# Sorting, placing and the first projections of a two-layer graph kernel in one block

## The reference, cut to what matters

```python
h = jnp.maximum(_layernorm(x, axis=-1), 0.0)
x = x + _L0_gnn_ref(h, src, dst, ...)        # two attention layers and two layer norms
h = jnp.maximum(_layernorm(x, axis=-1), 0.0)
x = x + _L1_gnn_ref(h, edge_index, edge_type_34, ...)   # means by relation, then GCN
# first attention layer, gatv2(h, ...):
fs = (x @ Ws + bs).reshape(-1, H, D)         # the two projections, 768 x 768 each
fd = (x @ Wd + bd).reshape(-1, H, D)
e = jax.nn.leaky_relu(fs[src] + fd[dst], 0.2)
logits = jnp.einsum('ehd,hd->eh', e, attn)
```

## Time and profile before

| | us |
|---|---|
| median of three executions | 3424.81 |
| the profiled execution | 3424.99 |
| its span | 3423.3 |
| TensorE busy | 2869.4 (84%) |
| VectorE busy | 2306.1 (67%) |
| ScalarE busy | 1693.3 (49%) |
| POOL busy | 1607.2 (47%) |

### The profile page before, as it was taken

The page is one execution under the profiler, slowest core; times in us unless marked ns, Lnnn a source line. Parts: engine busy times, 40 slices in busy tenths (PEclk is TensorE's granted clock), DMA queues, the critical chain, the costliest instruction groups (busy, mean ns, idle before and its releaser), DMA issues. The chain is left out here.

```text
span 3423.3 us, 59889 instructions
## 1 busy us (share of the span) xinstructions
PE 2869.4 (84%) x13554; PEld 2146.9 (63%) x13555; DVE 2306.1 (67%) x4378; ACT 1693.3 (49%) x5352; POOL 1607.2 (47%) x2067
## 2 busy tenths in 40 slices
PE   0396798889879799999676999999999995777799
PEld 0253455445445455555245999999999983555598
DVE  5234799999967688888475555555555547888743
ACT  0010799999932122333243656666566566777400
POOL 2473666566536555555112445544444445555201
PEclk6698899999989899999788999999999997989899
DMA  1332544444431355556226677777777746666411
GB/s 36 108 93 78 180 131 125 123 137 124 126 125 47 107 166 170 170 174 186 85 79 213 231 238 241 244 239 242 239 239 234 231 156 212 204 200 204 137 33 64
DMA packets 174949, 545.50 MB, mean 159 GB/s; under 512 B 55331, under 2 KB 56343, under 8 KB 174723
## 3 DMA queue, kind: packets, MB, share of 16 engines
q0 software_dynamic: 82000, 370.33, 34.5%
q1 hardware_dynamic: 72596, 128.39, 12.1%
q10 hardware_dynamic: 20304, 46.21, 4.3%
HBM read 461.31 MB, written 83.81 MB: 159 GB/s over the span
## 5 line engine op out<-in xcount | busy, mean ns | idle before, releaser
L2160 PE MATMUL pO<-wh,gT 128*128 128x384 f32 x3264 | 865.7, 339 | 22.9 <-ACT gT L2111 19.6
L770 POOL DMA_INDIRECT row<-fs_d,rec x400 | 463.3, 1158 | 392.1 <-PE pA L1295 167.8
L2160 PEld LDWEIGHTS pO<-wh,gT 128*128 128x128 f32 x3264 | 593.5, 188 | 32.1 <-ACT gT L2111 27.6
L2160 PE MATMUL pO<-wl,gT 128*128 128x384 f32 x1632 | 546.7, 335 | 0.0
L2174 DVE TENSOR_SCALAR cntge<-pT 128x768 int32<-128x768 int32 x137 | 131.2, 958 | 426.7 <-PE pT L485 234.0
L1003 ACT ACTIVATE sj<-sj 128x96 f32<-128x96 f32 x1176 | 313.2, 268 | 87.1 <-DVE sj L1120 85.9
L2111 ACT ACTIVATE gT<-cntge 128x256 fp32r<-128x256 f32 x822 | 295.3, 411 | 30.2 <-DVE cntge L2177 4.0
L2160 PEld LDWEIGHTS pO<-wl,gT 128*128 128x128 f32 x1632 | 307.7, 189 | 0.0
L770 POOL DMA_INDIRECT row<-y_d,rec x200 | 202.9, 1015 | 176.1 <-PE pR L2306 119.2
L2306 PE MATMUL pR<-row,share 128*128 128x384 f32 x384 | 169.5, 594 | 118.1 <-DVE acc L2354 65.8
L1042 PE MATMUL pS<-row,ident 128*128 128x384 f32 x400 | 179.2, 531 | 104.5 <-DVE sj L1120 64.3
(11 more groups left out here) (380 smaller groups left out, 5981.9 us busy)
## 6 DMA issues: line engine op xcount, KB each, us to landing
fdt<-in_L_gnn_W_rel_dram SPq DMA_DIRECT2D x170, 384.0 KB
startrow<-seen_d ACTq DMA_DIRECT2D x141, 320.0 KB
raw<-in_L_gnn_W_rel_dram SPq DMA_DIRECT2D x34, 384.0 KB
row<-fs_d,rec POOLq DMA_INDIRECT x400
kept_d<-fdt SPq DMA_DIRECT2D x10, 384.0 KB
kept<-kept_d SPq DMA_DIRECT2D x10, 384.0 KB
fs_d<-of SPq DMA_DIRECT2D x9, 388.0 KB
fd_d<-of SPq DMA_DIRECT2D x9, 388.0 KB
```

The source lines that it names most:

```text
L770: pool.indirect_dma_start(b["row"][u][:, j, :].bitcast(words), None, table, bass.IndirectOffsetOnAxis(ap=b["rec"][u][:, 2 * j + field:2 * ...
L2160: last = pe.matmul(pO[:, q, 0:HALF], gT[:, c, half, :].bitcast(F32R), w[:, c, lo:up].bitcast(F32R), start=c == 0 and k == 0, stop=c == KC ...
```

## The change

Stages 1, 2 and 3 become one stage with one block. The barriers between them and the clearing of semaphores there go. The helper functions (`halves` to `Signal`) move up unchanged. The buffers acc, den, cntge, rcnt and fdt are made after the merged stage instead of between the second and the third.

- SP: x(0,0) is loaded ahead of the edges, x(0,1) behind them; later loads and stores of the projections stand between the steps of the sorting.
- ScalarE issues the loads of the weights, biases and attention vector, ahead of its first norm. The weights have a semaphore each (w_in), the rest one together (v_in).
- POOL: the constants of placing and the empty row are made with the others; 20 marks ahead of the scatter by rank, 20 behind the all-reduce of the maxima, then the records and the three copies, then the last 60 marks.
- TensorE: turn(0,0) ahead of the degree matmuls, half of product(0,0) behind them, the other half behind the prefix matmuls, then tiles (0,1), (1,0) and (1,1) and the turn of (2,0), the placing, and from product(2,0) the loop as before.
- VectorE: norm(0,0) first; norm(0,1) while the degrees travel; evacuate(0,0) and norm(1,0) ahead of the rank passes; evacuate(0,1) and norm(1,1) behind them; evacuate(1,0) ahead of the wait for the maxima; norm(2,0) and evacuate(1,1) behind the tile table; then the placing and the rest.
- The sums of placing no longer have six PSUM banks. The matmuls with the triangle and with ones use the same place one after the other: two banks, and the free columns of pO[0]. So VectorE reads the first before TensorE makes the second, each read is two instructions, and the addition to `seen` comes ahead of the positions.

```diff
+                    load(0, 0, P)
                     sp.dma_start(dsti[:], e2(io["dst"])).then_inc(edges_in, 16)
...
+                    load(0, 1, P)
+                    sp.wait_ge(none_ok, 2)
+                    sp.dma_start(fs_d[0:1, :], none[:]).then_inc(none_out, 16)
                     sp.wait_ge(zero_ready, 1)
...
+                    load(1, 0, P)
+                    store(0, 0, P)
+                    load(1, 1, P)
                     sp.wait_ge(by_rank_out, 16 * NT)
...
+                    store(0, 1, P)
+                    load(2, 0, P)
+                    store(1, 0, P)
                     sp.wait_ge(tog_ready, 1)
...
+                    pool.wait_ge(recs_ready, 1)
+                    pool.wait_ge(clear, 16 + 16 * MARKS)
+                    mark_columns(0)
                     pool.wait_ge(ranks, 1)
...
                     pool.partition_all_reduce(kmax[:], degr[:, 0:NT], P, bass.bass_isa.ReduceOp.max).then_inc(maxima, 1)
+                    mark_columns(1)
+
+                    pool.wait_ge(recs_out, 16)
+                    pool.wait_ge(ctl_ok, 1)
+                    n = pool.value_load(ctl[0:1, C_RANKS:C_RANKS + 1], min_val=1, max_val=EC)
...
+                    for w, wn in enumerate(("L0_gnn_W1s", "L0_gnn_W1d")):
+                        act.dma_start(wt[w][:], w_view(io[wn])).then_inc(w_in[w], 16)
...
+                    pe.wait_ge(const_built, CONSTS)
+                    turn(0, 0, P)
                     pe.wait_ge(onehots, 1)
...
+                    hT_ok.wait(pe, 0, 0)
+                    pe.wait_ge(w_in[0], 16)
+                    half(0, 0, P, 0)
                     pe.wait_ge(deg_in, 32)
                     pe.matmul(p_pre[:, 0:NT], lower[:], keycol[:], start=True, stop=True)
                     pe.matmul(p_sum[:, 0:NT], ones[:], keycol[:], start=True, stop=True).then_inc(prefixes, 1)
+                    pe.wait_ge(w_in[1], 16)
+                    half(0, 0, P, 1)
+                    turn(0, 1, P)
+                    product(0, 1, P)
+                    turn(1, 0, P)
+                    product(1, 0, P)
+                    turn(1, 1, P)
+                    product(1, 1, P)
+                    turn(2, 0, P)
+                    pe.wait_ge(ctl_ok, 1)
...
+                        for place, lo, up in PLACES:
+                            last = pe.matmul(place[0:EP], lowb[:], onehot[:, lo:up], start=True, stop=True)
+                        last.then_inc(sums, 1)
+                        pe.wait_ge(sums_read, c * 2 + 1)
+                        for place, lo, up in PLACES:
+                            last = pe.matmul(place[0:EP], onesb[:], onehot[:, lo:up], start=True, stop=True)
+                        last.then_inc(sums, 1)
+                    pe.wait_ge(placed_all, 1)
+                    with pe.Fori(2, 4) as i:
...
+                    norm(0, 0, P)
                     v = Steps(dve, dve_step)
...
                     dve.sem_inc(deg_sb, 1)
+                    norm(0, 1, P)
                     dve.wait_ge(deg_in, 32)
...
+                    dve.wait_ge(v_in, 48)
+                    evacuate(0, 0, P)
+                    norm(1, 0, P)
                     for t in range(NT):
...
                     dve.sem_inc(ranks, 1)
+                    evacuate(0, 1, P)
+                    norm(1, 1, P)
                     dve.wait_ge(by_rank_in, 16)
...
+                    evacuate(1, 0, P)
                     dve.wait_ge(maxima, 1)
...
                     dve.sem_inc(tog_ready, 1)
+                    norm(2, 0, P)
+                    evacuate(1, 1, P)
...
-                        dve.wait_ge(sums, c + 1)
-                        w.link(dve.tensor_tensor(ahead[:], seen[:], p_low[0:EP].rearrange("p q f -> p (q f)")[:, 0:NP],
-                                                 ALU.add))
-                        w.link(dve.tensor_tensor(ahead[:], ahead[:], onehot[:], ALU.mult))
-                        w.link(dve.tensor_reduce(kcol[:], ahead[:], X, ALU.add))
+                        dve.wait_ge(sums, c * 2 + 1)
+                        with_places(dve, w, before, seen, ALU.add)
+                        dve.sem_inc(sums_read, 1)
+                        w.link(dve.tensor_tensor(before[:], before[:], onehot[:], ALU.mult))
+                        dve.wait_ge(sums, c * 2 + 2)
+                        with_places(dve, w, seen, seen, ALU.add)
+                        dve.sem_inc(sums_read, 1)
+                        w.link(dve.tensor_reduce(kcol[:], before[:], X, ALU.add))
...
-                        w.mark(dve.tensor_tensor(seen[:], seen[:], p_all[0:EP].rearrange("p q f -> p (q f)")[:, 0:NP],
-                                                 ALU.add))
+                    dve.sem_inc(placed_all, 1)
```

More of the change, by code:

```diff
@@ new lines, in _ @@
+                    c.mark(pool.memset(marks[:], 1.0))
+                    c.mark(pool.memset(ones[:], 1.0))
+                    c.mark(pool.iota(relbase[:, 0:RELS], [[NP, RELS]], base=1, channel_multiplier=0, **iota))
+                    c.mark(pool.memset(relbase[:, RELS:RELS + 1], BIG))
+                    c.mark(pool.iota(arow[:], [[1, DA]], base=0, channel_multiplier=0, **iota))
+                    c.mark(pool.memset(previ[0:1, 0:1], -1))
+                    c.mark(pool.memset(lower[:], 1.0))
@@ L666, in _ @@
                     copy(4, 1, LAST)
+                    for w in range(2):
+                        act.wait_ge(w_in[w], 16)
+                    act.wait_ge(v_in, 48)
                 @block.tensor
@@ L680, in product @@
                         for w in range(2):
-                            evac_ok.wait(pe, i, b - 1, w + 1)
-                            pe_product(pe, pO[w], hT[b], wt[w], rows).then_inc(prod_ok.sem, 1)
+                            half(i, b, rows, w)
+                    pe.wait_ge(const_built, CONSTS)
                     turn(0, 0, P)
-                    pe.wait_ge(w_in, 80)
-                    with pe.Fori(0, 4) as i:
+                    pe.wait_ge(onehots, 1)
+                    for c in range(EC):
+                        last = pe.matmul(p_deg[:, 0:DB], oa[:, c, :], ob[:, c, :], start=c == 0, stop=c == EC - 1)
@@ new lines, in _ @@
+                    for t in range(NT):
+                        v.link(dve.tensor_scalar(junk[:, 0:NP], keyrow[:], keycol[:, t:t + 1], 0.0, ALU.is_gt, ALU.add,
+                                                 accum_out=rank[:, t:t + 1]))
+                    v.link(dve.tensor_copy(ranki[:], rank[:]))
+                    dve.sem_inc(ranks, 1)
+                    evacuate(0, 1, P)
+                    norm(1, 1, P)
+                    dve.wait_ge(by_rank_in, 16)
+                    v.mark(dve.memset(perm[:, NT:NT + 1], NP - 1))
@@ new lines, in _ @@
+                    v.link(dve.tensor_scalar(junk[:], mrow[:], small[:, 3:4], 0.0, ALU.is_lt, ALU.add,
+                                             accum_out=small[:, 1:2]))
+                    v.mark(dve.tensor_scalar(ctl[0:1, C_TURNS:C_TURNS + 1], small[0:1, 1:2], 1.0, None, ALU.max))
+                    v.link(dve.memset(tog[:], 0.0))
+                    for t in range(NT):
+                        v.link(dve.scalar_tensor_tensor(out=tog[:], in0=gidx[:], scalar=gend[:, t:t + 1], in1=tog[:],
+                                                        op0=ALU.is_ge, op1=ALU.add))
@@ L728, in _ @@
+                    dve.sem_inc(placed_all, 1)
+                    with dve.Fori(2, 4) as i:
                         norm(i, 1, P)
```

575 lines of the change are left out of this document (270 added, 305 removed).

## The result

The changed kernel takes 3365.47 us (median of four executions, 3361.35 to 3369.07), the kernel before beside it 3423.53 (3420.76 to 3427.84): ratio 0.9829, 95% interval 0.9812 to 0.9846. The profiled execution took 3364.68 us, its span 3363.0. Between the two profiled executions that is -60.3 us, where -78.0 was forecast. The fall of 58 us is 1.7% and clear of noise. The 3347.0 is too low by 18 us, and the time lies just above the range, which ends at 3364.

The account below looks back on a forecast made before the run. TensorE's start on its last six tiles was taken to bound the region before the gather stage. Block -93.7 us, late start +8.5, configuration load +7.2: -78.0 from 3425.0 gives 3347.0 us, range 3333 to 3364.

Parts of the forecast that it names:

- the work behind 325 us: Everything from the gather stage on: taken to stay as it was and move as one block, apart from +7.2 us.
- degab at 36.4: VectorE's copy of the degrees in the sort: expected at its old time plus the +8.5 us start delay.
- part 2: Merged block up to VectorE's rank passes: two evacuation halves and a norm add 7.5 us, ranks at 66.0 plus s.
- s: Late start of the merged block: edge arrays held up by weight packets, +8.5 us, bounds +0.8 to +11.
- Rival (a): Start of the block: edge packets not held up, delay only 1 to 2 us, whole 3340; chance 20%.
- placing and the last six tiles: End of the block: onehot at 109.2, placed at 119.0, cold first product +2.8, last matmul at 224.3, all plus s.
- Rival (d): Last six products: TensorE's clock stays at 1.2 GHz from the placing on, 94 us more, whole 3441; chance 1%.
- the bill of the next stage: Gather stage's first iota: POOL's configuration load now falls there, on the path, +7.2 us, bounds 0 and 8.
- POOL's cover: End of the merged block: POOL has some 4.5 us in hand before SP's last store lands; longer delays paid in full.
- Rival (b): End of the block: POOL ends last, from its configuration load at the marks or longer marks, 3342 or 3355; chance 15%.
- Rival (c): VectorE in the sort: waits on half products fall on the chain, two evacuations some 10 us each, 3367; chance 8%.
- (e): Placing loop: the change doesn't do what it says because the loop runs many times; dismissed, no chance given.

Follow-up runs that it names:

- the two paddings: Changed kernel with 70 or 128 idle instructions added at the end of ScalarE's part of the merged block: ratios 0.9799 and 0.9819 of the kernel before.

## Why the prediction was right or wrong

The direction, the main mechanism and most terms held; the sum failed in one assumption and one unchanged piece. With only one of the two the time would have come out within the range. That it came only 1.5 us above it is partly luck: the stages behind attention were 4.8 us shorter, which nothing explains.

- **Failed: "The change keeps the work behind 325 us as it was; I take it to move as one block."** The work is the same, but ScalarE's program ahead of the attention loop grew (by 18 instructions, as counted), and 5 packets of instructions were fetched in each of its 12 turns. The stage took 11.5 us more in the profiled pair; 7.1 of them are shown by padding, 0.7 belong to the configuration load, and the rest is open. "If the gather stage itself changes its length" stood among what would make it wrong, but no rival had a price for it.
- **Failed: degab at 36.4**, which part 2 takes from the old lines plus s. It came at 40.80: 3.45 us for the late signals, whose cause stays open, and about 1 us for stalls in and behind the degree matmuls (0.43 and 0.45). On three chips it would have held (36.4 to 37.2).
- **Missed, small:** the degrees' round trip, 6.9 us from the end of their copy instead of 5.4, of which 0.9 come from x(1,0) and h(0,0) beside it (shown on another chip) and the rest is open; evacuation and norm together with the prefix part 8.3 instead of 7.5; 0.93 us of wait for a half product at the maxima, where product(1,0) ran 17.80 behind 6.28 us of idle; from togi to onehot 11.3 instead of 9.9. With the 4.4 above these make up the block's 9.8, but for a microsecond; 0.6 of that is the tile table (10.73 us from the maxima to togi, before 10.16).
- **Right: s.** ctl at 16.96 (17.3 forecast), and the cause was as told: with the weights asked for later, ctl is at 9.48. Rival (a) is out.
- **Right: placing and the last six tiles.** Onehot to product(2,0) 10.1 (9.8), the cold product 18.70 (+2.96, forecast +2.8), from there to the end of the last matmul 105.4 (105.3). Rival (d) is out: the second of the six already ran in 15.74.
- **Right: the bill of the next stage**, 7.94 for 7.2, and that its load would be at the iota. With the slower start behind it (0.7) the bill is 8.65 us up to the first gather of records, above the upper bound of 8.
- **Right, and thin as told: POOL's cover.** The last mark was done 4.3 us before SP's last store was issued; when an experiment put 5.6 us more on POOL, it ended last. Rival (b) had the mechanism, not here.
- Rival (c) gave 3367 and the time came near it, but for another reason: VectorE waited for products 0.93 us in the sort, not 20. (e) was rightly put aside.

## What to carry to other kernels

Code that is moved or added ahead of a long loop changes where the loop's instructions lie. When a stage that nobody touched gets longer by the same bit in each turn, look for idle time "issue" at one place per turn and at the packets of the instruction queue, and try some idle instructions as padding where the engine has nothing to do. Send small arrays that start the chain before the big ones are even asked for, across queues too. Price an unchanged piece from more than one chip if its size matters.

## What the runs showed of the hardware that was not expected

- ScalarE's loop of some 330 instructions fetches 5 packets of 8192 bytes per turn or none, by its position; a turn costs 0.5 us more (50.0 against 49.5) between the two paddings and 0.8 between the kernels before and after, with 2.5 and 2.8 us of idle time per turn ahead of the table load. The Trainium skill ("Runtime: NRT & Kernel Launch", on instruction fetch mechanics) says that blocks are fetched ahead and the cost is mostly hidden, but warns that a taken branch whose target isn't in the current window of two pages has to wait for a fetch. The traces agree with the warning, in that the loop has the packets and the idle time or neither; which branch waits, they don't show.
- POOL's configuration load (7.04 to 8.34 us over all profiles) also comes on the way back from the all-reduce to iota or tensor_tensor, and stood where the first of these was in every profile; copies, memsets and indirect DMAs don't call it.
- In seven profiles with the merged block, on chips with a slower kernel before, TensorE's signals behind 160 short matmuls came 3.3 to 4.3 us after the ends in the profile, and VectorE's row says "remote" there; in eleven on three other chips they came 0.01 us after. The ends are modelled: where a waiting engine starts much later than its releaser's row ends, the waiting engine is right.
